# Axial attention stage: packed keys, head pairs on the two halves of the array's rows, and outputs for eight heads at once

## Time and profile before

| | us |
|---|---|
| median of 3 runs | 2913.66 (2912.58 to 2915.99) |
| the profiled execution's own time | 2908.72 |
| its span | 2906.9 |
| PE busy in the span | 2467.0 |
| DVE busy | 1799.7 |
| ACT busy | 1248.9 |
| POOL busy | 297.7 |

### The profile page before, as it was taken

The page is one execution under the profiler, slowest core; times in us unless marked ns, Lnnn a source line. Parts: engine busy times, 40 slices in busy tenths (PEclk is TensorE's granted clock), DMA queues, the critical chain, the costliest instruction groups (busy, mean ns, idle before and its releaser), DMA issues. The chain is left out here.

```text
span 2906.9 us, 42566 instructions
## 1 busy us (share of the span) xinstructions
PE 2467.0 (85%) x15730; PEld 1904.7 (66%) x15746; DVE 1799.7 (62%) x5199; ACT 1248.9 (43%) x2982; POOL 297.7 (10%) x535
## 2 busy tenths in 40 slices
PE   5889999999974999799999999995888888883674
PEld 4668999998864999476667766763655555551332
DVE  6656767667875666445445544454566666657986
ACT  3434445444433211244344434452544444436663
POOL 3211100001000000000000000002111111101220
PEclk8999999999986999999999999997999999996887
DMA  4101211112005000000000000001000000003001
GB/s 156 62 23 41 70 37 40 69 36 74 29 26 194 1 1 1 1 1 1 1 1 1 1 1 1 1 1 51 5 5 5 5 5 5 5 1 133 1 1 58
DMA packets 41212, 83.41 MB, mean 29 GB/s; under 512 B 4528, under 2 KB 17840, under 8 KB 39856
## 3 DMA queue, kind: packets, MB, share of 16 engines
q1 hardware_dynamic: 41008, 80.70, 7.9%
HBM read 72.30 MB, written 8.39 MB: 28 GB/s over the span
## 5 line engine op out<-in xcount | busy, mean ns | idle before, releaser
L1990 DVE TENSOR_REDUCE s_nmax<-s_a_ps 128x2 f32<-128x512 f32 x256 | 174.3, 686 | 198.7 <-PE s_a_ps L1772 195.7
L651 ACT ACTIVATE s_p<-s_ms,s_nmax 128x256 f32<-128x256 f32 x256 | 128.5, 503 | 192.3 <-DVE s_nmax L754 192.3
L754 DVE CUSTOM_DVE_ANT_0 s_ms<-s_s_ps,s_bias 128x256 f32<-128x256 f32 x256 | 98.2, 421 | 175.9 <-PE s_s_ps L529 175.5
L1375 ACT ACTIVATE l_wo_w<-l_wo_w,s_nmax 128x128 f32<-128x128 f32 (+1 forms) x256 | 114.4, 447 | 197.8 <-DVE s_nmax L1471 197.0
L512 PE MATMUL s_q_ps<-s_xT,s_wh 128*128 128x256 f32 x1024 | 189.6, 286 | 0.0
L1215 PE MATMUL s_s_ps<-l_wqb_w,s_lT 128*128 128x512 f32 x384 | 175.7, 597 | 16.0 <-DVE l_wo_w L1441 15.3
L914 PE MATMUL s_h_ps<-s_xh,s_t 128*128 128x256 f32 x704 | 173.0, 284 | 9.3 <-DVE s_xl L1002 9.3
L1886 ACT ACTIVATE s_pT<-s_s_ps 128x512 f32<-128x512 f32 x256 | 151.6, 606 | 59.6 <-PE s_s_ps L1785 57.3
L562 PE MATMUL s_y_ps<-s_wh,s_oT 128*128 128x512 f32 x512 | 173.0, 399 | 0.0
L914 PE MATMUL s_h_ps<-s_xl,s_t 128*128 128x256 f32 x704 | 172.4, 283 | 0.0
L512 PEld LDWEIGHTS s_q_ps<-s_xT,s_wh 128*128 128x128 f32 x1024 | 165.5, 193 | 6.0 <-issue 0.5
(11 more groups left out here) (304 smaller groups left out, 6686.8 us busy)
## 6 DMA issues: line engine op xcount, KB each, us to landing
s_x_raw<-kept SPq DMA_DIRECT2D x24, 512.0 KB, 3.3
s_c_in<-in_ctx_T SPq DMA_DIRECT2D x32, 256.0 KB, 2.5
l_wqb_w<-in_l_xwq SPq DMA_DIRECT2D x4, 1024.0 KB, 7.8
l_wqb_w<-in_l_xwo SPq DMA_DIRECT2D x4, 1024.0 KB, 10.1
kept<-s_x_raw SPq DMA_DIRECT2D x8, 512.0 KB, 2.7
l_wo_w<-in_l_wo SPq DMA_DIRECT2D x1, 4096.0 KB, 15.5
s_raw<-in_l_w1T SPq DMA_DIRECT2D x2, 2048.0 KB, 9.9
s_raw<-in_l_w2T SPq DMA_DIRECT2D x2, 2048.0 KB, 21.5
```

Source lines behind the costliest of these rows:

```text
L651: act.activation(p[:, h % PR, q, :], ms[:, h % 2, q, :], ACT.Exp, scale=-1.0, bias=nmax[:, h % PR, q:q + 1], accum_out=den[:, h % PR, q:q ...
L754: dve.tensor_tensor_reduce(ms[:, h % 2, q, :], s_ps[:, h % 2, q * S:(q + 1) * S], bias[:, h // PER % B, :], -SCALE, 3.0e38, ALU.add, ALU.m ...
L1375: act.activation(p[:, h % PR, q, 0:(q + 1) * P], ms[:, h % 2, q, 0:(q + 1) * P], ACT.Exp, scale=-1.0, bias=nmax[:, h % PR, q:q + 1], accum ...
L1990: dve.tensor_reduce(nmax[:, g % 2, :, 2 * pair + e], a_ps[:, n % 2, :].rearrange("p (q k) -> p q k", q=QT), AX_X, ALU.max, negate=True).th ...
```

## The change

`kTz` is replaced by `kT` [128, 16, 256], in which a pair of heads shares the 128 rows as it does in q; a matmul for one head takes 64 rows only, the lower or the upper half of `qTx`, `qTm` and `kT`. PE's `greatest` and `scores` are called at even steps only, for both heads of a pair, in alternating order, and wait until both banks have been read. `outputs` is called once in eight steps and takes eight heads; `pT` holds sixteen heads. LAG, OUT_LAG and the steps of the projections move. ACT's exponentials and DVE's maxima stay one head a step. The fill with zeros goes.

```diff
-    LAG = GH + 3
-    QUADS = H // 4
-    QUAD_LAG = LAG + 3 + 2
-    OUT_LAG = QUAD_LAG + 5
+    LAG = GH + 4
+    PV_LAG = LAG + GH + 2
+    OUT_LAG = PV_LAG + 1
-    Q_AT, K_AT, V_AT, Y_AT = (10, 14), (19, 21), (12, 13), (16, 18)
+    Q_AT, K_AT, V_AT, Y_AT = (8, 11), (19, 21), (15, 16), (18, 20)
...
-        return n // GH, n % 4, n % GH // 4
+        return n // GH, n % GH // 2, n % 2
...
-        kTz = m.sb("kTz", [P, H, S], F32R)
+        kT = m.sb("kT", [P, H // 2, S], F32R)
-        pT = m.sb("pT", [P, GH, QT, S])
+        pT = m.sb("pT", [P, 2 * GH, QT, S])
...
-                pe.wait_ge(a_out, b * H + n + 1)
+                pe.wait_ge(a_out, b * H + n + 2)
                 for q in range(QT):
-                    mm = pe.matmul(a_ps[:, n % 2, q * S:(q + 1) * S], qTx[:, g % 2, pair, q * P:(q + 1) * P],
-                                   kTz[:, GH * g + 2 * pair + e, :], start=True, stop=True)
-                mm.then_inc(a_full, 1)
+                    for e in range(2):
+                        rows = slice(XD * e, XD * (e + 1))
+                        mm = pe.matmul(a_ps[:, e, q * S:(q + 1) * S], qTx[rows, g % 2, pair, q * P:(q + 1) * P],
+                                       kT[rows, PAIRS * g + pair, :], start=True, stop=True)
+                        if q == QT - 1:
+                            mm.then_inc(a_full, 1)
...
-                pe.wait_ge(s_out, (b + shift[whose]) * H + n + 1)
+                pe.wait_ge(s_out, (b + shift[whose]) * H + n + 2)
                 for k in range(QT):
-                    mm = pe.matmul(s_ps[:, n % 2, k * S:(k + 1) * S], kTz[:, GH * g + 2 * pair + e, k * P:(k + 1) * P],
-                                   qTm[:, g % 2, pair, :], start=True, stop=True)
-                mm.then_inc(s_full, 1)
+                    for e in range(2):
+                        rows = slice(XD * e, XD * (e + 1))
+                        mm = pe.matmul(s_ps[:, e, k * S:(k + 1) * S], kT[rows, PAIRS * g + pair, k * P:(k + 1) * P],
+                                       qTm[rows, g % 2, pair, :], start=True, stop=True)
+                        if k == QT - 1:
+                            mm.then_inc(s_full, 1)
...
+            def outputs(b, g):
+
+                pe.wait_ge(s_out, b * H + 2 + GH * (g + 1))
+                pe.wait_ge(o_out, b * G + g + 1)
+                for e in range(2):
+                    for k in range(QT):
+                        for part in range(2):
+                            for pair in range(PAIRS):
+                                ones_or_values = one[:, e, :] if part else v[:, k, GH * g + 2 * pair + e, :]
...
+                                mm = pe.matmul(o_ps[32 * pair:32 * pair + 32, part, :], ones_or_values,
+                                               pT[:, GH * (g % 2) + 2 * pair + e, k, :],
+                                               start=(e == 0 and k == 0 and part == 0),
+                                               stop=(e == 1 and k == QT - 1 and part == 1))
                 mm.then_inc(pv_done, 1)
...
                 for n in range(H):
-                    if has(b, "here"):
+                    if n % 2 == 0 and has(b, "here"):
                         greatest(b, n)
...
-                    if has(b, whose):
+                    if n % 2 == 0 and has(b, whose):
                         scores(b, whose, (n - LAG) % H)
...
-            act.copy(kTz[0:XD, 1::2, :], blank[0:XD, :].unsqueeze(1).broadcast_to([XD, H // 2, S])).then_inc(fixed, 1)
...
-                    heads = slice(GH * g, GH * (g + 1), 2)
-                    act.copy(kTz[0:XD, heads, cols], t[0:XD])
-                    heads = slice(GH * g + 1, GH * (g + 1), 2)
-                    act.copy(kTz[XD:P, heads, cols], t[XD:P]).then_inc(t_out, 1)
+                    act.copy(kT[:, PAIRS * g:PAIRS * (g + 1), cols], t).then_inc(t_out, 1)
...
-            dve.tensor_copy(kTz[XD:P, 0::2, :], blank[XD:P, :].unsqueeze(1).broadcast_to([XD, H // 2, S])).then_inc(fixed, 1)
```

More of the change, by code:

```diff
@@ L1816, in steps_of @@
                     whose = "prev" if n < LAG else "here"
-                    if has(b, whose):
+                    if n % 2 == 0 and has(b, whose):
                         scores(b, whose, (n - LAG) % H)
-                    whose = "prev" if n < QUAD_LAG else "here"
-                    if n % 4 == QUAD_LAG % 4 and has(b, whose):
-                        if whose == "here" and n == QUAD_LAG:
+                    whose = "prev" if n < PV_LAG else "here"
+                    if n % GH == PV_LAG % GH and has(b, whose):
+                        if whose == "here" and n == PV_LAG:
                             pe.wait_ge(f_out, f_turns.at(b, ("here", "v", QT - 1)) + 2)
-                        outputs(b + shift[whose], (n - QUAD_LAG) % H // 4)
+                        outputs(b + shift[whose], (n - PV_LAG) % H // GH)
                     for use in f_turns.steps[n]:
@@ L1834, in _ @@
                 project(0, n, "qk"[n // QT], n % QT, x_at=1)
-            pe.wait_ge(fixed, 4)
+            pe.wait_ge(fixed, 2)
             for n in range(2 * QT):
@@ L1854, in _ @@
                            ACT.Sin).then_inc(sines, 1)
-            act.wait_ge(fixed, 1)
-            act.copy(kTz[0:XD, 1::2, :], blank[0:XD, :].unsqueeze(1).broadcast_to([XD, H // 2, S])).then_inc(fixed, 1)
             def rows_over(at, bank, of, g, q):
@@ L1881, in exponentials @@
             def exponentials(b, j):
-                if j % 4 == 0:
-                    act.wait_ge(pv_done, b * QUADS + j // 4 + 1)
+                if j % GH == 0:
+                    act.wait_ge(pv_done, b * G + j // GH + 1)
                 act.wait_ge(s_full, b * H + j + 1)
-                act.activation(pT[:, j % GH, :, :], s_ps[:, j % 2, :].rearrange("p (k n) -> p k n", k=QT),
+                act.activation(pT[:, j % (2 * GH), :, :], s_ps[:, j % 2, :].rearrange("p (k n) -> p k n", k=QT),
                                ACT.Exp).then_inc(s_out, 1)
@@ L1899, in _ @@
                 rows_over(q, q % 2, "x", 0, q)
-            act.wait_ge(fixed, 4)
+            act.wait_ge(fixed, 2)
             for n in range(2 * QT):
@@ L1934, in _ @@
             dve.wait_ge(sines, 1)
-            dve.wait_ge(fixed, 1)
-            dve.tensor_copy(kTz[XD:P, 0::2, :], blank[XD:P, :].unsqueeze(1).broadcast_to([XD, H // 2, S])).then_inc(fixed, 1)
             for t in range(2):
@@ L1967, in values @@
                 if q == 0:
-                    dve.wait_ge(pv_done, b * QUADS + 2)
+                    dve.wait_ge(pv_done, b * G + 2)
                 t = f_ps[:, :].rearrange("p (h d) -> p h d", h=H)
@@ L1999, in sums_of_outputs @@
             def sums_of_outputs(b, g):
-                dve.wait_ge(pv_done, b * QUADS + 2 + 2 * g + 2)
+                dve.wait_ge(pv_done, b * G + 2 + g + 1)
                 dve.reciprocal(rden[:, :], o_ps[:, 1, :]).then_inc(rden_in, 1)
@@ L2033, in steps_of @@
                             step.end()
-            dve.wait_ge(fixed, 4)
+            dve.wait_ge(fixed, 2)
             dve.wait_ge(w_full, 5 * 16)
```

## The result

The changed kernel takes 3009.1 us (3006.7 to 3011.4), the kernel before 2914.0: 95 us more, a ratio of 1.0326 with a 95% interval from 1.0308 to 1.0344. The profiled execution took 3009.3 us with a span of 3007.4. The forecast was +49 us with a range up to 3005 us: the direction was right, the size half of what came, and 3009 lies above the range.

What follows compares the result with a forecast made beforehand. PE was taken to bound two thirds of a batch and DVE one third. Seven batches at +5.8 us, the ends and 5 us of clock gave +49 us, so 2962 us; own range 2937 to 2980, 8 in 10 2900 to 3005.

Steps and rivals of the forecast that it cites:

- PE's work: On PE: half-row groups save 5.4 us a batch, 44 more changes of shape cost 4.8; net 0.6 us less.
- rival 1: Half-row matmuls overlap fully and changes of shape are free: period 72 to 73 us, 2896 us in all; chance 0.17.
- What waits: PE and DVE waiting on banks filled and read in pairs: 81 us a batch against 75.2, 5.8 more.
- the walk: Step-by-step pricing of one batch: 24 us for steps 22 to 0, 57 for 0 to 22, sum 81.
- The clock: PE idling behind the layernorm's root brings one more half-clock stretch a batch, 0.7 us each (bounds 0 and 3), 5 in all.
- The ends: Outside the 7 full batches: the first batch +3 us, the last's end +1, the stage's start -1.
- The sum: 7 batches x 5.8 = 41, first 3, last's end 1, start -1, clock 5: +49 us.
- The rest: Single copy of k saves ACT time, -1 us at the start; zero fills cost nothing now; POOL and SP unchanged.
- Rival 2: Half-row matmuls don't overlap, or pauses lower the clock in DVE's third (`outputs` (30) +3.4 us): 85 us a batch, 2991; chance 0.2.

Runs made afterwards that it cites:

- e8b: Kernel before with packed keys, one copy of k and no zero fill, matmuls still over all 128 rows: 2911.7 us, ratio 0.9996.
- e4b: Changed kernel with the layernorm moved from steps 24, 26, 28 to 25, 27, 29, behind the odd head's maximum: 2988.5 us, ratio 1.0260.
- e10: Kernel before with the last batch's layernorm at steps 20, 21, 23 instead of 24, 26, 28: 2926.1 us, ratio 1.0039.

## What the prediction had right, and the step that failed

The waits came as walked. The term that failed is the clock's. In the order of the prediction's steps:

- **PE's work.** Priced at 0.31 us for a group of four and 0.11 for a change of shape, with 44 more changes. Between transposes a group takes 0.43 us and the transposes 0.47 (2289.95 to 2290.38 to 2290.85 below); by the prediction's prices they are 0.42 and 0.41. Full-row groups and transposes without a change take 0.24 and 0.30. So the change to half rows and back costs 0.36 for both, not 0.22, and the group itself is nearer to 0.24 than to 0.31, as rival 1 had it; the two errors nearly cancel, which is luck. Rival 1's free shapes did not come true. By the Trainium skill (TensorEngine Tiling, Key Properties) a change of tiling mode drains the engine: that agrees with these gaps.
- **What waits.** Counted from the changed trace's fills at 24, 0, 8, 16, 22 and again 24:

```profile
2279.71 0.51 PE L1773 MATMUL s_a_ps<-s_kT,s_qTx 64*128 64x256 f32 x4
...
2289.95 0.50 PE L1773 MATMUL s_a_ps<-s_kT,s_qTx 64*128 64x256 f32 x4
2290.38 0.54 PE L1734 MATMUL s_t_ps<-s_identr,s_kx 128*128 128x128 f32 x4
2290.85 0.50 PE L1789 MATMUL s_s_ps<-s_qTm,s_kT 64*128 64x256 f32 x4
...
2302.22 0.50 PE L1773 MATMUL s_a_ps<-s_kT,s_qTx 64*128 64x256 f32 x4
...
2323.58 0.50 PE L1773 MATMUL s_a_ps<-s_kT,s_qTx 64*128 64x256 f32 x4
...
2328.52 0.50 PE L1773 MATMUL s_a_ps<-s_kT,s_qTx 64*128 64x256 f32 x4
```

  Steps 0 to 8 took 17.0 us (2262.70 to 2279.71), the walk said 14.8; 8 to 16 took 22.5 against 21.8 to the end of v; 16 to 22 took 21.4 against 20.4; 22 to 0 took 4.9 + 20.4 = 25.3 against 24.1. The waits at 14, 16, 19, 20 and 21 were there, with 2.1, 1.2, 0.6, 1.3 and 0.5 us. In this batch the walk was short by 5.2 us.
- **The clock.** This is the step that failed: "I take one more such stretch a batch, at 0.7 us on the path (bounds 0 and 3)". The windows of the same batch show three stretches at the lower level, from 2246.4, 2266.9 and 2294.2, together 27 of 86 us:

```profile
2246.40:2260.00 13.60, 9.63 (x63) 6.64 (x67) 9.10 (x24) 6.21 (x11) 5.58 (x14) 0.50 0.01 2
2260.00:2266.90 6.90, 4.67 (x72) 2.89 (x64) 3.46 (x5) 1.57 (x3) 0.00 (x0) 0.99 0.00 0
2266.90:2277.10 10.20, 10.20 (x67) 7.15 (x69) 4.01 (x8) 7.38 (x13) 3.30 (x9) 0.50 0.01 2
2277.10:2294.20 17.10, 14.69 (x116) 8.07 (x108) 9.98 (x20) 5.81 (x11) 0.00 (x0) 1.00 0.00 0
2294.20:2297.60 3.40, 3.40 (x28) 1.95 (x30) 1.67 (x4) 1.67 (x3) 0.00 (x0) 0.50 0.02 5
2297.60:2331.70 34.10, 28.29 (x216) 14.69 (x208) 19.08 (x36) 9.17 (x17) 4.43 (x14) 1.00 0.03 8
```

  What this costs can be read from the blocks of outputs. At full clock a block takes 3.6 us, and the walk had 3.5. Over the six batches from 2089 to 2610, of the four blocks in a batch three, with one exception, start at half clock and take 4.4 to 5.8 us. That alone is 3.9 us a batch, above my bound of 3 for all of the clock. These blocks are on the path: DVE stands 4 us and more for each, and PE goes on right behind them without a pause. The clock is not the whole miss: steps 16 to 22 ran at full clock and took 1.0 us longer than walked. No run held the clock fixed, so the rest of its share is not shown.
- **The ends.** From the start of the last maxima's matmuls to the end of the stage it took 34.4 us before (2585.04 to 2619.46) and takes 44.3 now (2675.81 to 2720.09): 10 us more where I had 1.
- **The sum.** From batch 1 to batch 7 the fills at step 0 are 86.8 us apart on average (2088.56 to 2609.56), before 74.9 (2078.84 to 2528.14). That is 12.0 us more a batch, where walk and clock together had 5.8 + 0.7. Six such batches are 72 us (forecast 39), the last up to its last fill 9 (6.5), the first 5 (3), the start -2 (-1), the end 10 (1): 94 us, of 95 measured.
- **The rest.** That the single copy of k is worth nothing was in the forecast but for 1 us at the start; e8b confirms it.
- **Rivals.** Rival 2 had the right cause for its second half, a clock pulled down in the stretch that DVE sets, and at 2991 us was nearest to the 3009. It was too dear for `outputs` (30), +3.4 us where the batch shown has +0.8, and did not see that the blocks and steps outside that stretch run at half clock too.

By causes, as the runs separate them: the changed order 25 us (2911.7 to 2937.1), pairs with a wait for both banks 52 (to 2989.4), half rows 20 (to 3009.1). The split depends on the way through the runs. By the other way the half rows come first and cost 57 (2911.7 to 2969.2), the changed order 58 (to 3027.1), and the pairs then win 18 back (to 3009.1): on half rows two heads side by side save more than their wait for both banks costs.

## What to carry to other kernels

Taking two tiles at once halves the number of waits and doubles what each waits for: if both banks of a double buffer are filled together there is no double buffer any more. Where the pauses are followed by PE's lower clock they cost a second time, in the work behind them: price that work at both levels before adding up. The two halves of the array's rows do work side by side, but each change between half-row and other matmuls costs, so half rows are cheapest where they alternate and no other shape stands between them. No run here shows them paying: one head at a time on 64 rows was slower than on 128 rows with zeros, and in pairs they still cost 20 us. Put an engine's long work behind the instruction that frees the bank, not between two of them (e4b, 21 us).

## What the runs showed of the hardware

- 64-row matmuls of 256 columns, each with its own weights, start 0.12 us apart on one half of the rows, as full-row ones do, and 0.01 us apart on different halves. The first two behind another shape start 0.22 us apart on one half, and so they do at full rows.
- A change from 128-row to 64-row matmuls and back costs 0.36 us for both at full clock (0.43 + 0.47 against 0.24 + 0.30).
- In the batch shown of the changed kernel, PE's four pauses of 2.1 to 3.9 us each stood ahead of or within a stretch at half clock; in it a block of outputs took 4.4 us where at full clock it took 3.6.
- A kernel with one line of step numbers changed and less work on DVE (e10) ran 12 us longer, with PEclk at 0.95 instead of 0.98 in the steady stretch.
